# Product with V of an attention slot issued after both score steps of the slot, not between them

## The reference

```python
def _attn(q, k, v, mask):                      # block 0
    scale = 1.0 / np.sqrt(HD)
    s = jnp.einsum('bqhd,bkhd->bhqk', q, k) * scale
    s = jnp.where(mask, s, jnp.finfo(s.dtype).min)
    a = jax.nn.softmax(s, axis=-1)
    return jnp.einsum('bhqk,bkhd->bqhd', a, v)

x = _L0_xcond_ref(x, ...)   # self-attention, cross-attention, MLP
x = _L1_xcond_ref(x, ...)   # prototypes, router, three experts
x = _L2_xcond_ref(x, ...)   # self-attention, cross-attention, MLP
x = _L3_xcond_ref(x, ...)   # cross-attention, projection
```

## Time and profile before

| | before |
|---|---|
| median of 3 runs | 3509.27 us (3504.03 to 3510.4) |
| the profiled execution | 3505.52 us |
| its span | 3503.7 us |
| TensorE busy | 3300.4 us (94% of the span) |
| VectorE busy | 1840.0 us (53%) |
| ScalarE busy | 1436.5 us (41%) |
| GpSimd busy | 244.6 us (7%) |
| mean granted TensorE clock | 0.96 |

### The profile page before, as it was taken

How to read it: one execution, slowest core, us unless ns; L and a number is a source line. 1 busy time by engine, 2 the same in 40 slices (tenths; PEclk the granted TensorE clock), 3 DMA queues, 4 the chain that set the end, 5 groups by cost and what they waited for, 6 DMA issues and landing times.

```text
span 3503.7 us, 49090 instructions
## 1 busy us (share of the span) xinstructions
PE 3300.4 (94%) x19540; PEld 1823.4 (52%) x19540; DVE 1840.0 (53%) x3843; ACT 1436.5 (41%) x2607; POOL 244.6 (7%) x214
## 2 busy tenths in 40 slices
PE   6899999999889999998999999999999999999887
PEld 3555666657575666666433344534455344543364
DVE  4776544562412232324766775567755676556423
ACT  0344444344312222221355455554554645555333
POOL 1100100100100000001000010010100001010010
PEclk9999999989889999999899999999999999999898
DMA  5200000002000000001000000000000000000000
GB/s 166 90 6 1 8 20 4 25 1 95 16 22 1 0 1 0 1 1 55 1 1 1 1 7 4 1 25 7 7 4 16 10 7 7 4 16 16 1 1 13
DMA packets 57256, 57.99 MB, mean 17 GB/s; under 512 B 17728, under 2 KB 51248, under 8 KB 56764
## 3 DMA queue, kind: packets, MB, share of 16 engines
q1 hardware_dynamic: 57028, 54.79, 5.0%
HBM read 46.89 MB, written 7.89 MB: 16 GB/s over the span
## 4 chain that ended last, share of the span: by engine, by line
PE 89%; DVE 7%; ACT 2%; issue 1%; POOL 0%; DMA 0%; DVEq 0%; SPq 0%; ACTq 0%
PE ps L901 82%; PE ps L1075 3%; PE ps L1202 1%; DVE row_max_cross L1717 1%; PE ps L1055 1%; DVE max_halves L1564 1%; PE ps L1066 1%; ACT probs L1943 1%; DVE bn_stats L1618 1%; DVE xn_tok L1631 1%; DVE big L1723 1%; PE ps L1180 0%; ACT big L1895 0%; DVE bn_stats L1595 0%; DVE mean_var L1624 0%
## 5 line engine op out<-in xcount | busy, mean ns | idle before, releaser
L1895 ACT ACTIVATE big<-ps 128x512 f32<-128x512 f32 x1280 | 687.9, 598 | 795.1 <-PE ps L901 794.0
L901 PE MATMUL ps<-big 32*128 32x512 f32 (+2 forms) x5760 | 949.2, 603 | 15.9 <-DVE row_max L1561 4.3
L1564 DVE TENSOR_REDUCE max_halves<-ps 128x1 f32<-128x512 f32 x1024 | 653.0, 685 | 359.8 <-PE ps L901 359.0
L901 PEld LDWEIGHTS ps<-big 32*128 32x128 f32 (+1 forms) x5760 | 394.0, 188 | 497.5 <-issue 387.2
L901 PE MATMUL ps<-big,probs 128*32 128x512 f32 (+1 forms) x2688 | 378.7, 605 | 9.9 <-ACT big L1895 4.1
L901 PE MATMUL ps<-weights_mlp,big 128*128 128x256 f32 (+1 forms) x1248 | 334.7, 420 | 2.5 <-ACT big L1955 2.5
L901 PEld LDWEIGHTS ps<-weights_mlp,big 128*128 128x128 f32 x1248 | 235.4, 191 | 85.3 <-issue 57.0
L1601 DVE TENSOR_TENSOR x_tok<-ps,x_tok 128x512 f32<-128x512 f32 x112 | 77.4, 692 | 308.3 <-PE ps L901 308.3
L901 PE MATMUL ps<-x_T,weights_mlp 128*128 128x256 f32 x1024 | 229.6, 383 | 4.3 <-ACT x_T L1912 3.3
L1561 DVE TENSOR_REDUCE row_max<-ps 128x2 f32<-128x512 f32 x256 | 165.1, 686 | 128.0 <-PE ps L901 127.8
L1943 ACT ACTIVATE probs<-ps 77x512 f32<-77x512 f32 x384 | 196.4, 593 | 83.7 <-PE ps L901 83.7
(11 more groups left out here) (223 smaller groups left out, 3387.9 us busy)
## 6 DMA issues: line engine op xcount, KB each, us to landing
weights_mlp<-in_L_xcond_mlp_W SPq DMA_DIRECT2D x5, 1024.0 KB, 5.3
weights_mlp<-in_L_xcond_W_mlp SPq DMA_DIRECT2D x5, 1024.0 KB, 5.4
x_tok<-in_x SPq DMA_DIRECT2D x4, 1024.0 KB, 9.4
out_y<-x_tok SPq DMA_DIRECT2D x8, 512.0 KB, 2.9
big<-in_L_xcond_e_w SPq DMA_DIRECT2D x3, 1024.0 KB, 9.8
gates_biases<-mod_rows SPq DMA_DIRECT2D x20, 128.0 KB, 5.2
big<-in_L_xcond_adaLN_W SPq DMA_DIRECT2D x1, 2304.0 KB
kc_groups<-x_tok SPq DMA_DIRECT2D x3, 616.0 KB, 7.4
```

The source lines that it names most:

```text
L901: return pe.matmul(out, lhsT, rhs, start=first, stop=last)
L1564: dve.tensor_reduce(NMP[:, e, j, qt, hf:hf + 1], PS[:, bank, :], AX.X, ALU.max, negate=True).then_inc(R.frees(key), 1)
L1895: act.activation(PB[:, score % 2, j, :], PS[:, R.bank(key), :], ACT.Exp, scale=SCALE).then_inc(R.frees(key), 1)
```

## The change

In `slot` of TensorE, the call of `pv(product)` moves from the end of step 0 to the end of step 1.

```diff
@@ -1045,7 +1045,7 @@
                             scores(score, half)
                         for key in R.fills(fills, half):
                             fill(key)
-                        if half == 0 and product is not None:
+                        if half and product is not None:
                             pv(product)
                     for q in tails:
                         pe.wait_ge(R.acc, q + 1)
```

## The result

| | before | after |
|---|---|---|
| median of the runs | 3509.84 us (3504.03 to 3510.53, 4 runs) | 3636.85 us (3629.56 to 3645.19, 4 runs) |
| the profiled execution | 3505.52 us | 3629.56 us |
| its span | 3503.7 us | 3627.7 us |
| TensorE busy | 3300.4 us | 3411.2 us |
| mean granted TensorE clock | 0.96 | 0.96 |

The changed kernel takes 1.0358 times as long, with an interval of 1.0334 to 1.0381: 3.6% slower. The forecast had been 3583, so the direction was right, and the loss is 127 us where 77 were expected. The profiled executions differ by 124 us.

A forecast was written before the change was run, and what follows sets the result against it. TensorE was taken to bound the kernel. Slots +115 us, corrections +5 and -8, make +112; less 35 coming back gives +77, so 3505.5 becomes 3583 us, range 3550 to 3622.

The forecast's parts named there:

- What bounds the kernel: Whole kernel: TensorE, busy 94% of the span, sets the time; its waits lengthen it, though busy time doesn't show them.
- Step 1, the new wait: Step 1 of a slot: max1 waits some 0.86 us for sc0's bank; a lone slot takes 3.93 us.
- the formula: Each slot with scores and product: length is the end of its first exponential + 1.10 or 1.11 + 1.00 us.
- Step 2, the sum over slots: All 318 slots in three kinds: +71, +12 and +32 make +115; corrections +5 and -8 leave +112 us.
- the ring's part: Eight tiles of a full slot take seven banks, so the eighth waits for the first's exponential; +112 us over the slots.
- The end slots: 14 slots at the ends of the regions: no maxima, so no eighth tile; a correction of -8 us to the sum.
- The clock: Rival, 1700 to 3240 us: idle TensorE lowers the granted clock from 1.00 to 0.95, 77 us more, 3660; 5%.
- Step 3, what comes back: Stretches between slots: work behind a slot waits less; 35 us taken back, of at most 48.
- The range: Total time: 3550 if half as much more comes back, to 3622 if nothing does; the forecast has 80%.
- Faster: Rival, eighth tile: its bank is free in time, so 265 slots save 0.2 us each, 53 us, 3452; 3%.
- No difference: Rival, stretches between slots: the waits behind take nearly all 112 us back, 3505 to 3525; 5%.
- less than 40: Rival, stretches between slots: more comes back than the gaps show, slower by under 40 us, 3520 to 3550; 7%.

The follow-up runs named there:

- the short exponential: Changed kernel with each slot's first exponential over 32 of 512 columns from the third slot on: 3525.52 us; the same edit on the kernel before: 3497.99 us.
- The kernel with seven tiles: Changed kernel, product late, with the eighth tile max1 left out and VectorE reducing max0's bank twice: 3397.58 us, ratio 0.9686.
- the two kernels with seven tiles: Both leave out max1 and reduce max0's bank twice: the changed kernel (product late) 3397.58 us, the kernel before (product between the steps) 3449.83 us.
- the product put back in between: Changed kernel with the product between the steps again in the 22 slots that are first after an MLP step: 3596.47 us, ratio 1.0255.

## Why the prediction was right in kind and too small in size

**What bounds the kernel: right.** The time followed the starts on TensorE, and the busy column hid the new wait as it had hidden the old.

**Step 1, the new wait: right in each number.** Forecast 3.93 for a slot alone, load at 1.87, succession 3.93; measured 3.91, 1.87, 3.92. 199 of the 304 slots lie between 3.85 and 4.0 us. That the formula holds in its parts is shown by the short exponential: the load came 0.40 sooner and the slot was 0.39 shorter.

**Step 2, the sum over slots: the ring's part right, other waits left out.** The forecast for the slots was +112; by the same formula, with the exponentials as they ended in the new trace, it is +118. But the slots cost 158. The step that failed is the sentence that the new slot *is* the end of its first exponential plus 2.11. It is at least that. In 34 slots at full clock something ends later still, worth 17 us. In four more, in which the clock fell as well (236.59, 431.77, 741.34 and 2522.85 us), the slot is 3.2 to 3.8 us longer than the formula, 14 us in all, of which the half clock can have made no more than 5. The first of them waits for a bank that VectorE reads (weight loads, 241.74 us):

```profile
241.74 0.74 PEld L901 LDWEIGHTS ps<-big 32*128 32x128 f32 x8 [3.84 <-DVE x_T L1641]
```

The clearest of the 34 are those behind the query projection of the cross-attention (timeline of the changed kernel, 2010.45 us):

```profile
2010.45 2.00 PE L901 MATMUL ps<-big 32*128 32x512 f32 x12
2010.56 1.53 DVE L1589 TENSOR_SCALAR big<-ps,q_scale,group_bias 128x512 f32<-128x512 f32 x2 [3.93 <-PE ps L901]
...
2012.01 0.74 DVE L1705 TENSOR_SCALAR x_T<-ps,q_bias 128x512 f32<-128x512 f32 x1
...
2012.80 0.30 PEld L901 LDWEIGHTS ps<-big 32*128 32x128 f32 x4 [1.18 <-DVE x_T L1705]
...
2014.85 0.30 PEld L901 LDWEIGHTS ps<-weights,probs 128*128 128x128 f32 x2 [0.84 <-issue]
```

Here the seventh tile, max0, takes the bank of the last tile *ahead of* the slot, which VectorE still reads, busy with other reads until 2.3 after the slot's start: 4.40 us instead of 3.41. The early product had hidden that too. The kernel with seven tiles has the same wait at the same point (1900.75 us), 2.35 after the start, though nothing of its slot takes the bank of sc0:

```profile
1902.31 0.74 DVE L1709 TENSOR_SCALAR x_T<-ps,q_bias 128x512 f32<-128x512 f32 x1
...
1903.10 0.29 PEld L901 LDWEIGHTS ps<-big 32*128 32x128 f32 x2 [1.18 <-DVE x_T L1709]
```

I had looked only at the bank of sc0, when the change brings *all four* tiles of step 1 forward by a microsecond, and each has a bank of its own to be checked.

**The end slots: a term at nothing that was -21.5.** I took the 14 slots without maxima as neither longer nor shorter, since no eighth tile waits. That their two half-filled steps would merge into one, and that their product would stop waiting, I did not see, though both are readable in the kernel before.

**The clock: a rival at 5% that came true in part.** I argued from 1706 to 2003 us, where the clock stayed at 1.00 with a wait of some 0.8 us in most slots. That holds after the change too, as a window of the changed kernel shows:

```profile
1730.00:2040.00 310.00, 307.01 (x1832) 109.54 (x1826) 204.38 (x356) 154.82 (x293) 5.54 (x7) 1.00 0.00 1
```

But it says nothing of the 22 slots where the change makes the wait about 1.9 us, and leaves one tile in some 2.1. The slots with half clock inside account for some 26 us of the 40 beyond the formula (the 34 others are 17, the rest -3). Time at half clock can cost at most half of itself. By that I estimate that no more than 17 of these 26 are the clock, and at least 9 are waits, like the one at 241.74 above. And the rival's own size was far off: it had the clock from 1700 to 3240 us fall from 1.00 to 0.95, and it went from 0.99 to 0.98. The Trainium skill, "TensorE: Matmul & The Clock Gate", section "A second HAM failure mode: psum-queue depth-cycling", says that small idle times between matmul groups, with PSUM banks being cycled, can make the clock swing. This case agrees for the long waits (11 falls in 22) and does not for those of 0.7 to 0.9 us, which nearly every slot has.

**Step 3, what comes back: half of it.** 35 us were taken, 17 came. The bound of 48 was a sum of excess lengths, and I took most of it as waits for banks of the slot ahead. Some of what followed a slot was lengthened by the lower clock at the same time. How much would have come back without that was not separated, so this miss remains partly open.

**The range.** Its ends don't follow from its own words. Half as much more coming back is 52 us instead of 35, which gives 3565 and not 3550; nothing coming back is +112, which gives 3618 and not 3622. Above all, the range let only the give-back vary. The sum over the slots was taken as exact, and there the larger part of the miss lies.

By terms, against the forecast of +77: the ring's sum +6, what lies beyond it +40, the end slots -21.5, the give-back +17 or 18, the rest +5. That makes the 47 by which the profiled execution was missed. The other three runs of the changed kernel were longer than the profiled one at a slightly lower mean clock (3632.72, 3640.99 and 3645.19 us at 0.958, 0.956 and 0.954, the profiled one 0.959), which puts the median 7 us higher still.

**The rivals.** "Faster" lost because the bank isn't free at 0.96, as argued, and that its price of 53 us meets the 52 measured between the two kernels with seven tiles is luck. A slot where nothing waits did become shorter by the passage and the load (2.92 for 3.03 or 3.14). But only 56 of the 304 slots became some 0.2 shorter, not 265: the 304 together gained 10 us, the end slots 17 and the stretches between slots 24, which are terms of another kind. "No difference" and "less than 40" both rested on stretches between slots that would shrink, and these shrank by 17.

**Mode passages.** The Trainium skill, "TensorEngine Tiling (Array Packing)", section "Key Properties", says that a change of tiling mode empties the array. The trace agrees in sign: step to step is 0.96, step to product 1.07, and where nothing else waits, the order with one passage less is shorter, 2.92 for the slot and not 3.03.

## What to carry to other kernels

Work that stands between two takes of a ring of buffers is cover, even if it is never shown as waiting for anything. Before it is moved, count the tiles from take to take against the number of buffers, for each tile that comes forward and not for the first one only, and take the latest of the releases. Where a loop has iterations that differ (no maxima, a table load, another producer ahead), decide the order for each kind: the same move cost 0.9 us in one kind of slot here and gained 1.5 in another.

## What the runs showed of the hardware

- The granted clock fell from 2.4 to 1.2 GHz (0.57 in the mean from 3100 to 3104 us) after TensorE had run only one tile in some 2.1 us, within 3 us of the table load's end in 10 of the 21 cases; with the product put back in between, in none of them. With a wait of about 0.7 to 0.9 in each 3.9 us, over some 300 us, it stayed at 1.00 (1730 to 2040 us).
- A step with two of the four strips filled took as long as one with all four (3235.47 to 3236.52, 1.05, and 3233.98 to 3235.05, 1.07). With three filled it was no shorter either: the slot with seven tiles takes 1.93 for its two steps (3065.49 to 3067.42), twice the 0.96 of a full step.
- From the load of the late tile to the start of the next group it took 1.05 us at full clock in the kernels shown here, whatever had held the tile: 3246.39 to 3247.44 behind a 32-column exponential, 2260.19 to 2261.24 behind a table load, and 1.06 from 2012.80 behind VectorE, where the product starts at 2013.86.
